# Expert tiles of 256 slots instead of 512 in a two-expert routed block on one Trainium2 core

## The chip, the cores and the metric

The kernel is one program on one core of a Trainium2 chip. The metric is the device time of one launch in microseconds (us). TensorE (PE) multiplies matrices, VectorE (DVE) does elementwise work and reductions, ScalarE (ACT) evaluates the activation functions, GpSimd (POOL) does some elementwise work and issues the gathers and scatters, and SyncE (SP) issues all other transfers. The transfers of all issuers run on the core's 16 DMA engines.

## The reference

```python
x = L0_attn_x                                    # (2, 2048, 256) float32: 4096 tokens
x = x + attention(layernorm(x))                  # 16 heads, softmax plus a local band, projection
h = layernorm(x)
rh = gelu(h @ rW1 + rb1)                         # router, 256 -> 512
probs = softmax(rh @ rW2 + rb2)                  # 4 experts
weights, indices = top_k(probs, 2)               # each token goes to 2 of 4 experts
for e in range(4):                               # We1[e]: 256 -> 1024, We2[e]: 1024 -> 256
    yo = gelu(h * token_mask[e] @ We1[e] + be1[e]) @ We2[e] + be2[e]
    out = out + yo * combine_w[e]
x = x + out
```

4096 tokens times 2 experts make 8192 pairs of a token and an expert. Only these pairs are computed.

## The kernel before

Three stages follow one another: `project` (queries, keys), `attend` (attention, to about 1455 us) and `route_and_experts`. In the third, eight blocks of 512 tokens first run through projection, layer norm and router. For each token GpSimd scatters a row of 1056 bytes (the normalised token, its four gates, its number) to two slots of a DRAM table `xs`, which has one region per expert (`scatter`). The residual stream of each block is stored to `out` (`store_residual`).

Then come the expert tiles. A tile is a run of SLOTS = 512 slots of one expert. With 8192 pairs and 4 experts at most 8192/512 + 3 = 19 tiles (MOE_TILES) are needed, and always 19 are computed. Slots past an expert's last pair hold pads, whose token number is out of bounds, so that gathers and stores skip them. `list_tiles` writes for each tile its start row and its expert to `table`: `list_early` for the first EARLY = 5 tiles, which are full after the first sequence is routed, `list_late` for the others.

For tile i SyncE's `load_tile` issues four transfers in order: `xs` (the tile's rows, into one of two buffers), the first half of the expert's weights (L996, semaphore w1_in), the second half (L1001, w2_in), and the biases (L1007). Both halves of the weights are loaded anew for every tile, as pairs of float32r pieces (high and low part), into one of two buffers `w`. From tile 2 on each issue waits until the tile before the last has left the buffer: the first half waits for all eight `hidden` of tile i-2 (h_ready), the second for all eight `output` of it (h_used), the biases for the reading of its result (y_read). Since these waits stand in one queue, each also holds back what is issued behind it.

TensorE works in steps m = 0..7, one for each 128 of the 1024 hidden features. `hidden(i, m)` (L1509) is 6 matmuls over all the tile's slots, `output(i, m)` (L1528) has 3 matmuls of 256 columns for each 128 slots, so 12 for 512 slots. A step runs `hidden(i, m+2)` and then `output(i, m)`; in steps 6 and 7 the hidden parts are those of the next tile. `tile_transposes(i+1)` (L1495) stands at m = 4. Between the two, ACT's `gelu` (L1148) and DVE's `halves` (L1319 cast, L1321 subtraction) make the high and low pieces of the hidden values. The first `gelu` of a tile waits for the tile's biases. DVE also adds the output bias, multiplies by the gate and adds the gathered rows (`add_bias` L1331, `weigh_rows` L1339, `accumulate` L1346, at m = 1, 2, 3 of the next tile), and `prepare(i+1)` (L1305 to L1312, at m = 6) reads gates and token numbers; from i+1 = 2 on it waits until tile i-1 is stored. GpSimd's order is gather tile i (`gather_rows`, L1054, one indirect DMA for each 128 slots), store tile i (`store_rows`, L1062), gather tile i+1; every gather waits until the store of the tile before has landed, since both touch `out`.

The last block's routing (logits, choice of experts, counting, slots, `list_late`) is done beside the first steps of the expert tiles: the LAST_ and LATE_ numbers say at which step.

Of the kernel before, what the change touches and what calls it, by code (L numbers as in the profile page):

```python
# [29 lines left out]
P = 128  # L30
# [5 lines left out]
BT = 4  # L36
# [28 lines left out]
SLOTS = 512  # L65
# [3 lines left out]
XS_ROWS = EXPERTS * REGION + SLOTS  # L69
# [267 lines left out]
def attend(nc, ctx, dram, keep):  # L337
# [108 lines left out]
    def _(sp):  # L446
# [379 lines left out]
def route_and_experts(nc, ctx, dram, keep, block):  # L826
# [90 lines left out]
    ends = np.cumsum([0, BT * ROW, BT * ROW, SLOTS, SLOTS, MH + DIM, MH + DIM])  # L917
# [3 lines left out]
    y = [x_sb[:, HALF * BT:HALF * BT + BT, :], attnT[:].rearrange("p k (a f) -> p (k a) f", f=DIM)]  # L921
    rows = [o_st, v_st]
# [3 lines left out]
    xT = [(xT_hi0, sb("xT_lo0", [P, KD, SLOTS], F32R)[:]), (xT_hi[:], xT_lo[:])]  # L926
    gates = [sb(f"gates{u}", [P, BT, EXPERTS]) for u in range(2)]
    gate = [sb(f"gate{u}", [P, BT]) for u in range(2)]
    token = [sb(f"token{u}", [P, BT], U32) for u in range(2)]
# [18 lines left out]
    LAST_LOGITS, LAST_GATES, LAST_SLOTS, LATE_TABLE = 0, 1, 3, 4  # L948
# [66 lines left out]
    def _(pool):  # L1015
# [57 lines left out]
        pool.wait_ge(out_stored, 16 * BT * MOE_TILES)  # L1073

    @block.scalar
    def _(act):
# [74 lines left out]
        for i in range(MOE_TILES):  # L1151
            act.wait_ge(biases_in[i % 2], 16 * (i // 2 + 1))
            for m in range(MH):
# [3 lines left out]
                if i == 0 and m == LAST_GATES:  # L1157
# [3 lines left out]
    def _(dve):  # L1161
# [140 lines left out]
        def prepare(i):  # L1302
# [3 lines left out]
                                    chosen[:, i].unsqueeze(1).broadcast_to([P, BT, EXPERTS]), ALU.mult  # L1306
                                    ).then_inc(prep_step, 1)
            if i >= 2:
                dve.wait_ge(out_stored, 16 * BT * (i - 1))
# [14 lines left out]
        def add_bias(i):  # L1324
# [4 lines left out]
            elif i >= 2:  # L1329
                dve.wait_ge(out_stored, 16 * BT * (i - 1))  # L1330
            nc.vector.tensor_tensor(y[u], ps_y[u].rearrange("p b (t f) -> p (b t) f", f=DIM),  # L1331
                                    biases[u][:, MH:].unsqueeze(1).broadcast_to([P, BT, DIM]), ALU.add
                                    ).then_inc(y_read, 1)

        def weigh_rows(i):
# [3 lines left out]
            nc.vector.tensor_tensor(y[u], y[u], gate[u][:].unsqueeze(2).broadcast_to([P, BT, DIM]), ALU.mult  # L1339
                                    ).then_inc(y_gated, 1)  # L1340

        def accumulate(i):
            u = i % 2
            dve.wait_ge(y_gated, i + 1)
            dve.wait_ge(gathered, 16 * BT * (i + 1))
# [340 lines left out]
```

## Time and profile before

| | us |
|---|---|
| median of 3 runs | 2095.99 (2094.68 to 2101.74) |
| the profiled execution's own time | 2096.47 |
| its span in the trace | 2094.7 |
| first matmul of the expert tiles | 1627.87 |
| end of the last one | about 2080.5 |
| TensorE busy over the span | 2024.2 |

The span is what the trace covers; the execution's own time is 1.8 us longer. Times in rows are counted from the span's start. The stages share the engines in different ways, so busy shares of the whole span say little about the expert tiles; the rows below are of that stage.

### The profile page before, as it was taken

How to read it: one execution, taken by the hardware profiler on the slowest of the kernel's cores; microseconds unless marked ns; L12 is line 12 of the kernel's file. 1: busy time of each engine (PE TensorE's matmuls, PEld its weight loads, DVE VectorE, ACT ScalarE, POOL GpSimd, SP SyncE). 2: the span in 40 equal slices, each digit the busy share in tenths (PEclk: the TensorE clock that was granted, in tenths of full speed). 3: DMA queues.
4: the chain of work that ended last, by engine and by line, in shares of the span. 5: the costliest groups of instructions: out<-in, count | busy, mean ns of one | idle time of the engine just before them, and what ended most of it. 6: DMA issues, size and time to landing. Idle time of an engine off the chain costs nothing. (4 is left out here: it accounts for less than half of the span.)

```text
span 2094.7 us, 48471 instructions
## 1 busy us (share of the span) xinstructions
PE 2024.2 (97%) x16588; PEld 1083.5 (52%) x16588; DVE 1647.9 (79%) x2007; ACT 1402.4 (67%) x2502; POOL 392.9 (19%) x461
## 2 busy tenths in 40 slices
PE   7899999999999999999999999998998899999997
PEld 4443333333333333333333333333886799999996
DVE  6578999999999999999999999990355555565564
ACT  3227888888888888888888888888554322222221
POOL 1243001000100100010010001000044433334333
PEclk9888999999999999999999999999999999999998
DMA  7924434533543453354335335511124666776671
GB/s 261 243 52 92 90 71 90 120 72 72 118 93 71 89 118 76 71 113 99 71 86 119 78 71 106 106 49 31 52 97 179 243 249 239 267 264 242 232 266 54
DMA packets 102092, 267.69 MB, mean 128 GB/s; under 512 B 22894, under 2 KB 45936, under 8 KB 95344
## 3 DMA queue, kind: packets, MB, share of 16 engines
q1 hardware_dynamic: 91648, 241.25, 43.4%
q0 software_dynamic: 10368, 25.45, 3.5%
q8 instruction: 45, 0.74, 0.2%
q14 instruction: 31, 0.25, 0.0%
HBM read 212.87 MB, written 74.20 MB: 137 GB/s over the span
## 5 line engine op out<-in xcount | busy, mean ns | idle before, releaser
L588 DVE TENSOR_REDUCE part_max<-psum_attend 128x1 f32<-128x1024 f32 x1024 | 1241.0, 1221 | 81.8 <-PE psum_attend L710 65.5
L643 ACT ACTIVATE probs<-psum_attend 128x512 f32<-128x512 f32 x2048 | 1110.4, 596 | 155.0 <-PE psum_attend L723 149.6
L723 PE MATMUL psum_attend<-score_q,score_k 50*128 50x512 f32 x2048 | 756.1, 452 | 1.2 <-ACT v_sb L662 0.7
L710 PE MATMUL psum_attend<-max_k,max_q 48*128 48x512 f32 x2048 | 746.4, 454 | 8.8 <-PEq L1608 6.5
L735 PE MATMUL psum_attend<-probs,v_ones 128*32 128x256 f32 x8192 | 658.1, 393 | 9.3 <-ACT heads_sb L658 8.8
L723 PEld LDWEIGHTS psum_attend<-score_q,score_k 50*128 50x128 f32 x2048 | 308.9, 186 | 409.8 <-ACT probs L643 395.9
L735 PEld LDWEIGHTS psum_attend<-probs,v_ones 128*32 128x32 f32 x8192 | 162.5, 108 | 386.0 <-issue 202.8
L710 PEld LDWEIGHTS psum_attend<-max_k,max_q 48*128 48x128 f32 x2048 | 296.9, 187 | 23.8 <-issue 13.6
L1148 ACT ACTIVATE x_sb<-psum_route,x_sb 128x512 f32<-128x512 f32 x152 | 104.5, 689 | 287.0 <-PE psum_route L1509 243.8
L1528 PE MATMUL psum_route<-w,h_hi 128*128 128x256 f32 x1216 | 218.5, 279 | 2.4 <-DVE h_lo L1321 1.3
L1528 PEld LDWEIGHTS psum_route<-w,h_hi 128*128 128x128 f32 x1216 | 195.8, 189 | 16.6 <-issue 1.7
L1319 DVE CAST h_hi<-x_sb 128x512 fp32r<-128x512 f32 x152 | 65.3, 430 | 132.8 <-ACT x_sb L1148 115.3
L1528 PE MATMUL psum_route<-w,h_lo 128*128 128x256 f32 x608 | 169.3, 278 | 0.0
L549 POOL CAST shift<-neg_max 128x16 fp32r<-128x16 f32 x31 | 6.1, 196 | 592.2 <-DVE neg_max L596 592.2
L1528 PEld LDWEIGHTS psum_route<-w,h_lo 128*128 128x128 f32 x608 | 114.7, 189 | 0.2 <-issue 0.2
L1321 DVE TENSOR_TENSOR h_lo<-x_sb,h_hi 128x512 fp32r<-128x512 f32 x152 | 105.4, 693 | 5.2
L1509 PE MATMUL psum_route<-w_end,w 128*128 128x512 f32 x320 | 102.3, 401 | 2.9 <-ACT x_sb L1148 2.9
L1509 PE MATMUL psum_route<-route_xT_hi,w 128*128 128x512 f32 x288 | 91.6, 399 | 0.0
L514 POOL COPY v_ones<-v_sb 128x256 f32<-128x256 f32 x32 | 12.7, 397 | 337.3 <-PE psum_attend L735 337.1
L1032 POOL DMA_INDIRECT xs<-xrow,slot_at x64 | 62.9, 984 | 29.9 <-issue 18.1
L559 POOL TENSOR_TENSOR o_sb<-heads_tok,inv_sum 128x256 f32<-128x256 f32 x33 | 20.4, 620 | 252.5 <-DVE inv_sum L604 221.2
L1062 POOL DMA_INDIRECT out<-x_sb,token x40 | 40.9, 1024 | 109.6 <-DVE x_sb L1346 98.4
(171 smaller groups left out, 1538.0 us busy)
## 6 DMA issues: line engine op xcount, KB each, us to landing
w<-w_split SPq DMA_DIRECT2D x38, 2048.0 KB
max_q<-qk_pieces SPq DMA_DIRECT2D x192, 128.0 KB, 7.4
score_k<-qk_pieces SPq DMA_DIRECT2D x192, 128.0 KB, 4.6
xs<-in_pads SPq DMA_DIRECT2D x33, 528.0 KB, 5.8
qk_pieces<-pieces SPq DMA_DIRECT2D x32, 512.0 KB, 4.6
w_split<-w_pair SPq DMA_DIRECT2D x32, 512.0 KB, 6.3
max_k<-qk_pieces SPq DMA_DIRECT2D x192, 64.0 KB, 7.6
score_q<-qk_pieces SPq DMA_DIRECT2D x192, 64.0 KB, 2.2
```

The costliest lines, as they stand in the source:

```text
L588: nc.vector.tensor_reduce(part_max[:, t, p:p + 1], ps_m[p].rearrange("q b f -> q (b f)"), axis=AXIS.X, op=ALU.max).then_inc(m_read, 1)
L643: nc.scalar.activation(probs[kb % 2][:, chunk * BLOCK:(chunk + 1) * BLOCK], bank_of(at), ACT.Exp, scale=float(HD) ** -0.5).then_inc(exp_do ...
L710: last = nc.tensor.matmul(ps_m[p][:, h, :], max_q[u][rows, t * P:(t + 1) * P], max_k[u][rows, p * BLOCK:(p + 1) * BLOCK], start=True, stop ...
L723: nc.tensor.matmul(bank_of(at), score_k[u][rows, kb * P:(kb + 1) * P], score_q[u][rows, part * BLOCK:(part + 1) * BLOCK], start=True, stop ...
L735: last = nc.tensor.matmul(ps_o[QUAD * j:QUAD * (j + 1), at:at + BLOCK // PARTS], v_ones[u][:, kb, :], probs[kb % 2][:, j * BLOCK + at:j * ...
L1032: nc.gpsimd.indirect_dma_start(dram["xs"], bass.IndirectOffsetOnAxis(ap=at, axis=0), xrow[i % XROWS][:, t, :], None).then_inc(scattered[i ...
L1062: nc.gpsimd.indirect_dma_start(dram["out"], bass.IndirectOffsetOnAxis(ap=token[u][:, t:t + 1], axis=0), y[u][:, t, :], None, bounds_check= ...
L1148: nc.scalar.activation(h[m % H], ps_h[m % PS_H], ACT.Gelu, bias=biases[i % 2][:, m:m + 1]).then_inc(gelu_done, 1)
L1319: nc.vector.tensor_copy(h_hi[m % HALVES], h[m % H]).then_inc(h_hi_ready, 1)
L1321: nc.vector.tensor_tensor(h_lo[m % HALVES], h[m % H], h_hi[m % HALVES].bitcast(F32), ALU.subtract).then_inc(h_lo_ready, 1)
L1509: last = nc.tensor.matmul(ps_h[m % PS_H], w[u][:, 2 * k + m // 4, c, at:at + P], xx[:, k, :], start=j == 0, stop=j == len(terms) - 1)
L1528: last = nc.tensor.matmul(ps_y[u][:, t // 2, (t % 2) * DIM:(t % 2 + 1) * DIM], hs[m % HALVES][:, toks], w[u][:, chunk, c, at:at + DIM], st ...
```

## The change

Tiles have 256 slots. There are then 8192/256 + 3 = 35 of them, and EARLY is 4096/256 - 3 = 13. Every operation over a tile's slots has half the width or half the count; weights and biases are loaded once for each tile as before. The result of a tile takes half a PSUM bank group, and `output(1, 0)` no longer shares a bank with the counting, so one wait goes. The last block's routing is spread over more steps, now counted across tiles. The filling of `xs` with pads keeps its 33 transfers of 512 rows.

```diff
-SLOTS = 512
+SLOTS = 256
+PADS = 512
...
-XS_ROWS = EXPERTS * REGION + SLOTS
+XS_ROWS = EXPERTS * REGION + PADS
...
-            sp.dma_start(dram["xs"][ds(n * SLOTS, SLOTS), :], dram["pads"]).then_inc(pads_in, 16)
+            sp.dma_start(dram["xs"][ds(n * PADS, PADS), :], dram["pads"]).then_inc(pads_in, 16)
...
-    ps_x = psum[:, 2:4, :]
-    ps_h = [psum[:, 4 + c, :] for c in range(PS_H)]
-    ps_y = [psum[:, 6:8, :], psum[:, 0:2, :]]
+    ps_x = psum[:, 2:4, 0:SLOTS]
+    ps_h = [psum[:, 4 + c, 0:SLOTS] for c in range(PS_H)]
+    ps_y = [psum[:, 6, :], psum[:, 1, :]]
...
-    LAST_LOGITS, LAST_GATES, LAST_SLOTS, LATE_TABLE = 0, 1, 3, 4
+    LAST_LOGITS, LAST_GATES, LAST_COUNT, LAST_SLOTS, LATE_TABLE = 0, 2, 3, 6, 10
...
-                pool.wait_ge(out_stored, 16 * BT * i)
+                pool.wait_ge(out_stored, 16 * ST_TILES * i)
...
-            for t in range(BT):
+            for t in range(ST_TILES):
...
-                if i == 0 and m == LAST_GATES:
+                if MH * i + m == LAST_COUNT:
                     exponentials(BLOCKS - 1)
...
-                elif m == LAST_LOGITS:
+                if MH * i + m == LAST_LOGITS:
                     read_logits(BLOCKS - 1)
-                elif m == LAST_GATES:
+                elif MH * i + m == LAST_GATES:
                     choose(BLOCKS - 1)
-                elif m == LAST_SLOTS:
+                elif MH * i + m == LAST_SLOTS:
                     weigh(BLOCKS - 1)
                     give_slots(BLOCKS - 1)
-                elif m == LATE_TABLE:
+                elif MH * i + m == LATE_TABLE:
                     list_late()
...
-                elif i == 1:
-                    pe.wait_ge(place_read, BLOCKS)
-                else:
+                elif i >= 2:
                     pe.wait_ge(y_read, i - 1)
             pe.wait_ge(h_lo_ready, s + 1)
             chunk, at = W1 + m // 2, (m % 2) * DIM
-            for t in range(BT):
+            for t in range(ST_TILES):
...
-                if i == 0 and m == LAST_GATES:
+                if MH * i + m == LAST_COUNT:
                     count_slots(BLOCKS - 1)
```

TensorE's queue around steps 0 and 1 of tile 0, before. `w_end` and `xT_lo` are the high and low pieces of the tile's transposed rows, `w` the weights, `h_hi` and `h_lo` the pieces of the hidden values.

```order
L1509 MATMUL psum_route<-w_end,w 128x512 [waits gelu_done]
L1509 MATMUL psum_route<-w_end,w 128x512
L1509 MATMUL psum_route<-xT_lo,w 128x512 x2
L1509 MATMUL psum_route<-w_end,w 128x512 x2
L1528 MATMUL psum_route<-w,h_hi 128x256 [waits h_lo_ready]
L1528 MATMUL psum_route<-w,h_hi 128x256
L1528 MATMUL psum_route<-w,h_lo 128x256
L1528 MATMUL psum_route<-w,h_hi 128x256 x2
L1528 MATMUL psum_route<-w,h_lo 128x256
L1528 MATMUL psum_route<-w,h_hi 128x256 x2
L1528 MATMUL psum_route<-w,h_lo 128x256
L1528 MATMUL psum_route<-w,h_hi 128x256 x2
```

The same place with the change (lines are numbered two higher up to `output`):

```order
L1511 MATMUL psum_route<-w_end,w 128x256 [waits gelu_done]
L1511 MATMUL psum_route<-w_end,w 128x256
L1511 MATMUL psum_route<-xT_lo,w 128x256 x2
L1511 MATMUL psum_route<-w_end,w 128x256 x2
L1528 MATMUL psum_route<-w,h_hi 128x256 [waits h_lo_ready]
L1528 MATMUL psum_route<-w,h_hi 128x256
L1528 MATMUL psum_route<-w,h_lo 128x256
L1528 MATMUL psum_route<-w,h_hi 128x256 x2
L1528 MATMUL psum_route<-w,h_lo 128x256
```

The hidden part keeps its six matmuls at half the columns; the output part keeps its 256 columns and has six matmuls for twelve.

SyncE's queue of one tile (tile 2) before, with what each transfer waits for; the names are those of `load_tile`.

```order
L992 ISA [waits prepared,x_tr]
L992 DMA x_sb<-xs 128x4x264
L996 ISA [waits h_ready]
L996 DMA w<-w_split 128x4x1024
L1001 ISA [waits h_used]
L1001 DMA w<-w_split 128x4x1024
L1007 ISA [waits y_read,gelu_done]
L1007 DMA x_sb<-in_be 128x264
```

The same with the change:

```order
L994 ISA [waits prepared,x_tr]
L994 DMA x_sb<-xs 128x2x264
L998 ISA [waits h_ready]
L998 DMA w<-w_split 128x4x1024
L1003 ISA [waits h_used]
L1003 DMA w<-w_split 128x4x1024
L1009 ISA [waits y_read,gelu_done]
L1009 DMA x_sb<-in_be 128x264
```

Order and waits are the same; only the tile's rows are halved, the two halves of the weights keep their size, and the list now stands 35 times for 19.

## Rows read from the trace of the kernel before

**Rows 1.** The page's part 1: busy us (share of the span) xinstructions of each engine.
```profile
PE 2024.2 (97%) x16588; PEld 1083.5 (52%) x16588; DVE 1647.9 (79%) x2007; ACT 1402.4 (67%) x2502; POOL 392.9 (19%) x461
```
**Rows 2.** DMA issues, 1500 us on: out<-in, queue, kind, count, KB each.
```profile
w<-w_split SPq DMA_DIRECT2D x38, 2048.0 KB
x_sb<-xs SPq DMA_DIRECT2D x19, 528.0 KB
x_sb<-in_be SPq DMA_DIRECT2D x19, 132.0 KB
```
**Rows 3.** Windows view: stretch, length, busy of PE, PEld, DVE, ACT, POOL, PEclk, DMA share, GB/s.
```profile
1800.00:1900.00 100.00, 100.00 (x660) 90.69 (x659) 58.70 (x101) 28.24 (x39) 37.99 (x36) 1.00 0.70 253
```
**Rows 4.** Timeline of SP's queue: start us, us, engine, line, operation; both weight halves.
```profile
1731.43 0.38 SPq L996 DMA_DIRECT2D w<-w_split  x1
1738.33 0.38 SPq L1001 DMA_DIRECT2D w<-w_split  x1
...
1754.42 0.38 SPq L996 DMA_DIRECT2D w<-w_split  x1
```
**Rows 5.** Windows view, shorter stretches.
```profile
1610.00:1636.00 26.00, 21.55 (x121) 15.82 (x120) 9.63 (x43) 13.37 (x17) 14.40 (x15) 0.96 1.03 405
...
1748.00:1752.00 4.00, 4.00 (x32) 3.75 (x31) 1.96 (x3) 2.08 (x3) 2.60 (x3) 1.00 0.30 109
...
1780.00:1784.00 4.00, 4.00 (x30) 3.71 (x29) 1.35 (x3) 1.38 (x2) 1.34 (x2) 1.00 1.02 411
```
**Rows 6.** Timeline of all engines inside the expert tiles.
```profile
1740.36 0.43 DVE L1319 CAST h_hi<-x_sb 128x512 fp32r<-128x512 f32 x1 [0.47 <-ACT x_sb L1148]
...
1740.75 0.63 PE L1509 MATMUL psum_route<-w_end,w 128*128 128x512 f32 x2
...
1740.82 0.69 DVE L1321 TENSOR_TENSOR h_lo<-x_sb,h_hi 128x512 fp32r<-128x512 f32 x1
...
1742.13 0.40 PE L1528 MATMUL psum_route<-w,h_hi 128*128 128x256 f32 x2
...
1742.33 0.69 ACT L1148 ACTIVATE x_sb<-psum_route,x_sb 128x512 f32<-128x512 f32 x1 [2.07 <-PE psum_route L1509]
...
1743.51 0.63 PE L1509 MATMUL psum_route<-w_end,w 128*128 128x512 f32 x2
...
1749.03 1.03 PE L1495 MATMUL psum_route<-ident_sb,x_sb 128*128 128x128 f32 x8
...
1749.82 0.71 PE L1509 MATMUL psum_route<-w_end,w 128*128 128x512 f32 x2
```
**Rows 7.** Timelines of PE and SP at the start of the expert tiles.
```profile
1607.83 10.11 SPq L996 DMA_DIRECT2D w<-w_split  x1
...
1637.01 1.22 PE L1509 MATMUL psum_route<-w_end,w 128*128 128x512 f32 x2 [2.87 <-ACT x_sb L1148]
...
1660.55 0.38 SPq L996 DMA_DIRECT2D w<-w_split  x1
```
**Rows 8.** PE's timeline and a half-microsecond window in the routing stage.
```profile
1481.91 1.93 PE L1436 MATMUL psum_route<-ident_sb,xrow 128*128 128x128 f32 x8 [1.68 <-DVE xrow L1293]
...
1482.50:1483.00 0.50, 0.50 (x5) 0.50 (x4) 0.00 (x0) 0.00 (x0) 0.00 (x0) 0.50 0.01 4
```
**Rows 9.** Timeline of the end: result of the last tile on DVE, its stores on POOL.
```profile
2080.63 1.22 DVE L1331 TENSOR_TENSOR x_sb<-psum_route,x_sb 128x1024 f32<-128x1024 f32 x1 [2.15 <-PE psum_route L1528]
...
2083.15 1.22 DVE L1346 TENSOR_TENSOR x_sb<-x_sb,o_st 128x1024 f32<-128x1024 f32 x1
2085.22 1.03 POOL L1062 DMA_INDIRECT out<-x_sb,token  x1 [3.86 <-DVE x_sb L1346]
...
2089.15 0.99 POOL L1062 DMA_INDIRECT out<-x_sb,token  x1 [0.30 <-issue]
```
**Rows 10.** Timeline of POOL: last store of a tile, first gather of the next.
```profile
1750.23 0.99 POOL L1062 DMA_INDIRECT out<-attnT,token  x1 [0.30 <-issue]
...
1753.54 1.05 POOL L1054 DMA_INDIRECT o_st<-out,token  x1 [2.33 <-DMA out<-attnT,token]
```

More of the change, by code:

```diff
@@ L916, in route_and_experts @@
     x_at = x_sb[:].rearrange("p t f -> p (t f)")
-    ends = np.cumsum([0, BT * ROW, BT * ROW, SLOTS, SLOTS, MH + DIM, MH + DIM])
+    ends = np.cumsum([0, ST_TILES * ROW, ST_TILES * ROW, SLOTS, SLOTS, MH + DIM, MH + DIM])
     xs0, xs1, h0, h1, biases0, biases1 = (x_at[:, int(a):int(b)] for a, b in zip(ends, ends[1:]))
@@ L920, in route_and_experts @@
     h, biases = [h0, h1], [biases0, biases1]
-    y = [x_sb[:, HALF * BT:HALF * BT + BT, :], attnT[:].rearrange("p k (a f) -> p (k a) f", f=DIM)]
-    rows = [o_st, v_st]
+    y = [x_sb[:, HALF * BT:HALF * BT + ST_TILES, :],
+         attnT[:].rearrange("p k (a f) -> p (k a) f", f=DIM)[:, 0:ST_TILES, :]]
+    rows = [o_st[:, 0:ST_TILES, :], v_st[:, 0:ST_TILES, :]]
     h_hi = [sb(f"h_hi{c}", [P, SLOTS], F32R)[:] for c in range(HALVES)]
@@ L925, in route_and_experts @@
     xT_hi0 = keep["w_end"][:, 0:KD * SLOTS].rearrange("p (k n) -> p k n", k=KD)
[L926 to L929, printed above, removed]
+    xT = [(xT_hi0, sb("xT_lo0", [P, KD, SLOTS], F32R)[:]), (xT_hi[:, :, 0:SLOTS], xT_lo[:, :, 0:SLOTS])]
+    gates = [sb(f"gates{u}", [P, ST_TILES, EXPERTS]) for u in range(2)]
+    gate = [sb(f"gate{u}", [P, ST_TILES]) for u in range(2)]
+    token = [sb(f"token{u}", [P, ST_TILES], U32) for u in range(2)]
     full = sb("full", [P, EXPERTS])
@@ L1072, in _ @@
             store_rows(i)
-        pool.wait_ge(out_stored, 16 * BT * MOE_TILES)
+        pool.wait_ge(out_stored, 16 * ST_TILES * MOE_TILES)
     @block.scalar
@@ L1305, in prepare @@
             nc.vector.tensor_tensor(gates[u][:], xs[u][:, :, GATE_AT:GATE_AT + EXPERTS],
[L1306 removed]
+                                    chosen[:, i].unsqueeze(1).broadcast_to([P, ST_TILES, EXPERTS]), ALU.mult
                                     ).then_inc(prep_step, 1)
             if i >= 2:
[L1309 removed]
+                dve.wait_ge(out_stored, 16 * ST_TILES * (i - 1))
             dve.wait_ge(prep_step, 2 * i + 1)
@@ L1329, in add_bias @@
             elif i >= 2:
-                dve.wait_ge(out_stored, 16 * BT * (i - 1))
-            nc.vector.tensor_tensor(y[u], ps_y[u].rearrange("p b (t f) -> p (b t) f", f=DIM),
-                                    biases[u][:, MH:].unsqueeze(1).broadcast_to([P, BT, DIM]), ALU.add
+                dve.wait_ge(out_stored, 16 * ST_TILES * (i - 1))
+            nc.vector.tensor_tensor(y[u], ps_y[u].rearrange("p (t f) -> p t f", f=DIM),
+                                    biases[u][:, MH:].unsqueeze(1).broadcast_to([P, ST_TILES, DIM]), ALU.add
                                     ).then_inc(y_read, 1)
@@ L1493, in tile_transposes @@
             for k in range(KD):
-                for t in range(BT):
+                for t in range(ST_TILES):
                     last = nc.tensor.transpose(ps_x[:, k, t * P:(t + 1) * P], xs[u][:, t, k * P:(k + 1) * P], ident[:])
@@ L1524, in output @@
             chunk, at = W1 + m // 2, (m % 2) * DIM
-            for t in range(BT):
+            for t in range(ST_TILES):
                 toks = slice(t * P, (t + 1) * P)
                 for j, (hs, c) in enumerate(((h_hi, 0), (h_hi, 1), (h_lo, 0))):
-                    last = nc.tensor.matmul(ps_y[u][:, t // 2, (t % 2) * DIM:(t % 2 + 1) * DIM],
+                    last = nc.tensor.matmul(ps_y[u][:, t * DIM:(t + 1) * DIM],
                                             hs[m % HALVES][:, toks], w[u][:, chunk, c, at:at + DIM],
-                                            start=m == 0 and j == 0 and t % 2 == 0,
-                                            stop=m == MH - 1 and j == 2 and t % 2 == 1)
+                                            start=m == 0 and j == 0 and t == 0,
+                                            stop=m == MH - 1 and j == 2 and t == ST_TILES - 1)
             last.then_inc(h_used, 1)
@@ L1648 @@
     j, e = np.arange(EXPERTS)[None, :], np.arange(EXPERTS)[:, None]
-    pads = np.zeros((SLOTS, ROW), np.float32)
+    pads = np.zeros((PADS, ROW), np.float32)
     pads[:, ID_AT] = TOKENS
```

4 lines of the change are left out of this document (2 added, 2 removed).

## The prediction

> **What bounds the kernel now.** I read the page first: TensorE is busy for 2024.2 of 2094.7 us [rows 1], but that mixes three stages, and the change touches only the last 450 us. So I went to the windows view of that stage, then to SP's queue and to the timeline of one tile. In the middle of the expert tiles TensorE is busy for 100 of 100 us at full clock, VectorE for 59, ScalarE for 28, and the 16 DMA engines for a share of 0.70, moving 253 GB/s [rows 3]. The stage is bound by TensorE, and the reader should see the second number too: the transfers have only 30% in hand. The first weight halves of two successive tiles are issued at 1731.43 and 1754.42 [rows 4]: a tile of 512 slots takes 23.0 us.
>
> Inside a tile the hidden part of a step takes 1.38 us (1740.75 to 1742.13) and the output part 1.38 us (to 1743.51) [rows 6]. That is 0.230 us for a matmul of 512 columns and 0.115 us for one of 256: time goes with the columns, and a matmul of 256 columns pays nothing for its own weight load. The eight transposes take 0.79 us (1749.03 to 1749.82) [rows 6]. So 8 x 2.76 + 0.8 = 22.9 us.
>
> **The change, part by part.** *TensorE's work.* A step of 256 slots is 6 + 6 matmuls of 256 columns, 12 x 0.115 = 1.38 us; a tile is 8 x 1.38 + 0.4 = 11.45 us. There are 35 for 19: 35 x 11.45 = 401 us against 19 x 23.0 = 437 us. The 36 us are the pads that are no longer computed (9728 slots become 8960). If nothing else were there, this would be the gain.
>
> *The transfers.* What a tile loads for its slots is halved, what it loads for its expert is not: 2 x 2048 KB of weights and 132 KB of biases [rows 2], for 11.45 us of TensorE work instead of 23. A full tile of 256 slots moves 4.19 MB of weights, 0.135 MB of biases, 0.27 MB of rows (half of 528 KB [rows 2]), and gathers and stores 256 rows of 1 KB each, 0.52 MB: 5.12 MB. In 11.45 us that is 447 GB/s. Before it was 253 [rows 3]. What can the DMA engines do? In the one long stretch in which they are never without work, 26 us at the start, they move 405 GB/s with scatters of 1 KB rows in the mix; in weights alone 411; in gathers alone 109 GB/s at a share of 0.30, so 360 for a full share [rows 5]. None reaches 447. The bound therefore passes from TensorE to the transfers. For the mix of 82% weights and 18% small rows I take 395 GB/s, between 0.82 at 405 with 0.18 at 350 (about 394) and the 405 of the long stretch: 13.0 us for a full tile, where TensorE needs 11.45.
>
> The Trainium skill, page "DMA: Bandwidth & Descriptors", section Specifications, puts HBM's limit for one core at about 358 GB/s. The trace disagrees: 405 GB/s over 26 us [rows 5]. By the page's figure the stream below would take 470 us instead of 426, and the span would be 2144 us.
>
> *Is the stream fed?* The change alters no wait, but every wait now comes twice as often. Call b the moment at which the biases of tile i are there; they are queued behind its second weight half, and the first gelu needs them. Then gelu 0 and the two operations of `halves` follow, at 256 columns between half and all of 0.69, 0.43 and 0.69 us [rows 6]; I take 0.5, 0.27 and 0.43, with 0.2 for the handovers: `output(i,0)` starts at b + 1.4. From there to `output(i,7)` TensorE has 15 parts of 0.69 and the transposes, 10.8 us: b + 12.2. The next b' is at b + 13.0. TensorE waits for about 1 us a tile. `hidden(i,7)` is done at b + 8.7, which releases the first half for tile i+2; at that time the second half of tile i+1 is still under way, to b + 12.5. The second half for tile i+2 is released at b + 12.2, with the first still before it. So something is always queued, with about 4 us in hand, and a late TensorE catches up before the queue runs dry. SP's issue can block while the queue is full (10.11 us [rows 7]); that costs nothing here, since it happens only while the engines have work.
>
> *ScalarE and VectorE.* Gelu to `halves` must fit in the four parts between `hidden(i,m)` and `output(i,m)`, 2.76 us; the chain is about 1.2 us plus 0.6 for handovers, and an extra operation of VectorE adds 0.69. It fits, with less than 1 us in hand. `prepare(i+1)` at m = 6 waits for the stores that follow `accumulate` at m = 3: 0.85 us from VectorE to GpSimd (2084.37 to 2085.22 [rows 9]), two issues 2.3, landing 2.3 (1751.22 to 1753.54 [rows 10]), together 5.5 us after `accumulate`, where three steps and the split are about 4.5. VectorE stalls there for about 1 us, up to 3 if stores land late beside weights. TensorE's 1 us of waiting hides the first; the rest would come on top only if it passed the 4 us above in every tile. I cost it at nothing and keep 13.6 us a tile as the upper end (rival 3).
>
> *The clock.* After a wait of TensorE of 1.68 us the granted clock was 0.50, its level of 1.2 GHz [rows 8]. With a wait in every tile this can happen. A slow stretch makes TensorE late, the wait vanishes, and so does the cause; as long as the transfers bound the tile it costs nothing.
>
> *The start.* Before, `hidden(0,2)` starts at 1637.01 and the first weight half of tile 2 is issued at 1660.55 [rows 7]: 23.5 us, of which six steps are 16.6 and about 7 are the last block's routing, the slow clock there and stalls. With the change six steps are 8.3 us and I keep the 7: with the start 0.5 us earlier, 1652. If the spreading hides all the 7 it is 1645, if it costs 12 it is 1657. The late table and the waits of tile 1 fall in the time in which tile 2 is loaded; I add 1 us for a gap in the stream, and 1 us until the first bytes flow.
>
> *The sum.* From there the tiles 2 to 34 are one stream: 33 x (4.194 + 0.135 + 0.270) = 151.8 MB, and 16.3 MB of the 16.8 MB that 8192 pairs gather and store: 168.1 MB at 395 GB/s are 425.6 us. The stream ends at 1652 + 2 + 425.6 = 2079.6, b is 0.5 later. Then 1.4 us to the first output part, 13 parts of 0.69 = 9.0, three VectorE operations of 0.69 with 0.2 between them, 0.85 to GpSimd, 2.3 for two stores, and 4.6 from there to the end as before (2090.14 to 2094.7 [rows 9]): 20.4 us. The span is 2100.5, against 2094.7; with the 1.8 us around it the time is 2102. The profiled execution took 2096.47, the median is 2095.99, so nothing is to be corrected. The gain of TensorE, 36 us, is thus all given back and 6 us more.
>
> **The rivals.**
> 1. *The stream is faster, and the kernel too.* This decides from 408 GB/s on. For it: 411 in weights alone and 405 in the long mix [rows 5]. Against it: stretches with gathers beside weights are below that. At 409 GB/s the stream is 411 us, and with a start at 1650 the span is 2084, the time 2086.
> 2. *The stream is slower.* In steady state 253 GB/s at a share of 0.70 are 361 GB/s for a full share [rows 3], because a transfer holds its engines while it starts and ends. If back-to-back transfers keep that loss, 168.1 MB take 466 us, and the time is 2142. Against it: the long stretch has the same starts and ends and reaches 405. At 380, half way, the time is 2119.
> 3. *The step chain or the stores bound the tile.* VectorE's wait for `out_stored`, with late landings and a slow clock, makes a tile 13.6 us and leaves gaps in the stream: 33 x 13.6 = 449, the time 2125. For it: the chain has less than 1 us in hand, the clock fell after 1.68 us [rows 8]. Against it: the 4 us that are queued ahead.
> 4. *The change does only what it says:* TensorE stays the bound with 11.45 us a tile, the time is 2062. It needs 447 GB/s, more than any row shows.
>
> **How the numbers follow.** Forecast (the transfers bound at about 395 GB/s, 2093 to 2111): 0.45. Rival 1: 0.18. Rival 2: 0.17. Rival 3: 0.15. Rival 4: 0.02. Left over 0.03. A measurement of this kernel can tell 0.3%, 6.3 us: same is 2089.7 to 2102.3. The forecast lies at its upper edge, so of its 0.45 I give 0.20 to same and 0.25 to slower; of rival 1 0.15 to faster and 0.03 to same; rivals 2 and 3 are slower but for 0.01 each. Slower 0.56, same 0.25, faster 0.19. The range leaves out rival 4 and the far end of rival 2: 2083 to 2130; the forecast's own is 2093 to 2111.
>
> **What would show it.** Right: in the middle of the expert tiles the DMA share is near 1 and 385 to 405 GB/s, the first weight halves are issued 12.6 to 13.4 us apart, TensorE is busy for 85 to 92 of 100 us and waits once a tile, at the biases or w2_in. The first half for tile 2 is issued between 1645 and 1657, and from the last second half to the end there are about 21 us. Wrong: TensorE busy for 100 of 100 (rival 4, or the chain), a DMA share of 0.9 or less with longer tiles (rival 3), a share of 1 at 360 GB/s (rival 2).

## The result, and the profile after

The changed kernel takes 2238.65 us (median of 4 runs, 2224.51 to 2249.21), the one before beside it 2095.34 (2086.1 to 2101.74): a ratio of 1.067, with an interval of 1.063 to 1.072. I had forecast 2102, with a range to 2130. The sign was right; of 143 us lost I had foreseen 6.

The page of the changed kernel first: part 1, one issue line, part 4 (the chain that ended last) and the group of part 5 that stands for `prepare`.

```profile
PE 2055.6 (92%) x17200; PEld 1147.1 (51%) x17200; DVE 1682.4 (75%) x2375; ACT 1432.8 (64%) x2646; POOL 388.3 (17%) x449
...
DMA 10%; issue 3%; POOL 2%; DVE 1%; PE 0%; POOLq 0%; ACT 0%; DVEq 0%
...
L1313 DVE TENSOR_REDUCE gate<-gates 128x2 f32<-128x8 f32 x35 | 5.6, 161 | 140.5 <-DMA out<-x_sb,token 72.3
...
w<-w_split SPq DMA_DIRECT2D x70, 2048.0 KB
```

TensorE's share has gone from 97% [rows 1] to 92%, there are 70 weight halves for 38 [rows 2], and TensorE has 0% of the chain that ended last. VectorE stands idle for 140.5 us before 35 tiny reductions that cost 5.6: they are the ones behind `prepare`'s wait, the wait that I had costed at nothing. It is about the size of the loss.

SP's queue at the start and the end of the stream:

```profile
1653.68 0.38 SPq L998 DMA_DIRECT2D w<-w_split  x1
...
2194.18 0.38 SPq L998 DMA_DIRECT2D w<-w_split  x1
```

The stream starts where it was expected (1653.68, forecast 1652). From there to the first half of tile 34 are 540.5 us for 32 tiles: 16.9 us a tile, not 13.0. The windows view in between (columns as in [rows 3]):

```profile
1700.00:2200.00 500.00, 399.61 (x2951) 391.36 (x2952) 250.23 (x684) 129.70 (x266) 128.69 (x120) 0.89 0.83 300
```

This is the picture that I had named for rival 3: a DMA share under 0.9 with longer tiles. Nothing is full. TensorE works 80% of the time, the transfers 83%, at 300 GB/s. When no engine is the bound, the next thing to look for is a loop of waits. The timelines of POOL and DVE for one turn of it, with the idle time and its releaser in brackets:

```profile
1778.51 1.17 POOL L1056 DMA_INDIRECT v_st<-out,token  x1 [5.48 <-DVE token L1314]
1779.97 1.13 POOL L1056 DMA_INDIRECT v_st<-out,token  x1 [0.30 <-issue]
1788.19 1.03 POOL L1064 DMA_INDIRECT out<-attnT,token  x1 [7.09 <-DVE attnT L1348]
1789.53 1.00 POOL L1064 DMA_INDIRECT out<-attnT,token  x1 [0.31 <-issue]
```

```profile
1777.65 0.16 DVE L1313 TENSOR_REDUCE gate<-gates 128x2 f32<-128x8 f32 x1 [5.10 <-DMA out<-x_sb,token]
...
1786.67 0.69 DVE L1348 TENSOR_TENSOR attnT<-attnT,v_st 128x512 f32<-128x512 f32 x1 [2.15 <-DMA v_st<-out,token]
...
1795.28 0.16 DVE L1313 TENSOR_REDUCE gate<-gates 128x2 f32<-128x8 f32 x1 [5.22 <-DMA out<-attnT,token]
```

From one `gate` to the next are 17.6 us: 0.86 to the first gather, 2.59 for two issues, **5.57 until the gathered rows have landed**, 0.69 for `accumulate`, 0.83 to GpSimd, 2.34 for two stores, **4.75 until they have landed**. Tile i+1 cannot be gathered before tile i is stored, and tile i cannot be stored before it was gathered, so the loop turns once a tile whatever TensorE does. The profile names VectorE's `token` as what releases the gather, because it comes last; by the code the gather and `gate` wait for the same landing, and the 0.86 us are GpSimd's own start. Before, the loop also turned once a tile, but a tile lasted 23 us, and the gather came 2.33 us after the last store [rows 10], where here it comes 5.60 us after (1790.53 to 1796.13).

That this loop closes can be read from `accumulate`: it waits for its gathered rows in nearly every tile. Waits view, 1650 to 2238 (engine, tile and line, releaser: us in total, times, longest):

```profile
DVE x_sb L1348 <- DMA o_st<-out,token: 36.9, 17, 3.6
...
DVE attnT L1348 <- DMA v_st<-out,token: 33.1, 15, 3.9
```

What it does to TensorE: VectorE, held at `gate`, has the next pieces of the hidden values behind it. The same view:

```profile
PE psum_route L1528 <- DVE h_lo L1323: 107.3, 41, 6.3
...
DVE gate L1313 <- DMA out<-x_sb,token: 72.3, 16, 7.9
DVE gate L1313 <- DMA out<-attnT,token: 68.0, 16, 6.5
```

PE's timeline at the turn shown above, and windows of one microsecond before and after:

```profile
1796.22 0.80 PE L1528 MATMUL psum_route<-w,h_hi 128*128 128x256 f32 x2 [3.62 <-DVE h_lo L1323]
```

```profile
1794.00:1795.00 1.00, 0.00 (x0) 0.00 (x0) 0.00 (x0) 0.00 (x0) 0.00 (x0) 1.00 1.03 418
1797.00:1798.00 1.00, 1.00 (x7) 1.00 (x6) 0.89 (x3) 0.00 (x0) 0.69 (x2) 0.50 0.53 205
```

At 1794 TensorE, VectorE, ScalarE and GpSimd all stand still until one store has landed, while the weights of a later tile run at 418 GB/s. After 3.62 us of idle time the granted clock is 0.50, TensorE's level of 1.2 GHz, as after the 1.68 us of [rows 8]. The mean over 500 us is 0.89.

### The profile page after: what moved, and what is told of

Same layout as the page of the kernel before. It is cut to its first block and busy times, and to the rows that moved or that the text cites. A ratio compares the mean times of both kernels' runs of the same rounds, so it can differ in the third digit from the quotient of the medians.

```text
span 2238.0 us, 50903 instructions
## 1 busy us (share of the span) xinstructions
PE 2055.6 (92%) x17200; PEld 1147.1 (51%) x17200; DVE 1682.4 (75%) x2375; ACT 1432.8 (64%) x2646; POOL 388.3 (17%) x449
## 5 line engine op out<-in xcount | busy, mean ns | idle before, releaser
L1150 ACT ACTIVATE x_sb<-psum_route,x_sb 128x256 f32<-128x256 f32 x280 | 132.9, 475 | 406.7 <-PE psum_route L1511 240.1
L1528 PE MATMUL psum_route<-w,h_hi 128*128 128x256 f32 x1120 | 238.5, 307 | 111.7 <-DVE h_lo L1323 107.3
L1321 DVE CAST h_hi<-x_sb 128x256 fp32r<-128x256 f32 x280 | 88.6, 316 | 60.5 <-ACT x_sb L1150 53.6
L1511 PE MATMUL psum_route<-w_end,w 128*128 128x256 f32 x576 | 126.5, 304 | 2.7 <-ACT x_sb L1150 2.7
L1323 DVE TENSOR_TENSOR h_lo<-x_sb,h_hi 128x256 fp32r<-128x256 f32 x280 | 120.1, 429 | 9.7
L1511 PE MATMUL psum_route<-route_xT_hi,w 128*128 128x256 f32 x544 | 118.4, 301 | 1.3 <-ACT x_sb L1150 1.3
L1313 DVE TENSOR_REDUCE gate<-gates 128x2 f32<-128x8 f32 x35 | 5.6, 161 | 140.5 <-DMA out<-x_sb,token 72.3
L1511 PEld LDWEIGHTS psum_route<-w_end,w 128*128 128x128 f32 x576 | 98.2, 209 | 3.9 <-ACT x_sb L1150 2.9
L1511 PEld LDWEIGHTS psum_route<-route_xT_hi,w 128*128 128x128 f32 x544 | 92.0, 208 | 1.5 <-ACT x_sb L1150 1.5
L515 POOL COPY v_ones<-v_sb 128x256 f32<-128x256 f32 x32 | 12.7, 397 | 336.8 <-PE psum_attend L736 336.7
```

The costliest lines, as they stand in the source:

```text
L1150: nc.scalar.activation(h[m % H], ps_h[m % PS_H], ACT.Gelu, bias=biases[i % 2][:, m:m + 1]).then_inc(gelu_done, 1)
L1321: nc.vector.tensor_copy(h_hi[m % HALVES], h[m % H]).then_inc(h_hi_ready, 1)
L1323: nc.vector.tensor_tensor(h_lo[m % HALVES], h[m % H], h_hi[m % HALVES].bitcast(F32), ALU.subtract).then_inc(h_lo_ready, 1)
L1511: last = nc.tensor.matmul(ps_h[m % PS_H], w[u][:, 2 * k + m // 4, c, at:at + P], xx[:, k, :], start=j == 0, stop=j == len(terms) - 1)
L1528: last = nc.tensor.matmul(ps_y[u][:, t * DIM:(t + 1) * DIM], hs[m % HALVES][:, toks], w[u][:, chunk, c, at:at + DIM], start=m == 0 and j = ...
```

## The experiments

**Without the round trip.** Stores go to a table of their own, gathers don't wait for them, and four buffers of token numbers take `prepare`'s wait away. The store itself now waits for the store before it.

```diff
-    token = [sb(f"token{u}", [P, ST_TILES], U32) for u in range(2)]
+    token = [sb(f"token{u}", [P, ST_TILES], U32) for u in range(4)]
...
-                pool.wait_ge(out_stored, 16 * ST_TILES * i)
...
+            if i > 0:
+                pool.wait_ge(out_stored, 16 * ST_TILES * i)
...
-                nc.gpsimd.indirect_dma_start(dram["out"],
+                nc.gpsimd.indirect_dma_start(dram["acc"],
...
-            if i >= 2:
-                dve.wait_ge(out_stored, 16 * ST_TILES * (i - 1))
+            if i >= 4:
+                dve.wait_ge(out_stored, 16 * ST_TILES * (i - 3))
```

> From the changed kernel: the tiles' results are stored to a tensor of their own, while the gathers read `out`, which after the routing nobody writes any more; so a gather no longer waits for the store before it (the store itself waits, before it is issued, until the one before has landed), and four buffers of gates and token numbers take away VectorE's wait in `prepare`. It leaves out that the two experts' results of a token are added up. Same transfers, same bytes, same engine work. Theory A (the tile is bound by the ring gather, landing, accumulate, store, landing, prepare, gather, 17.1 us): with the ring cut the transfers bound the tile at 13.0 us, time 2095 to 2115 us, DMA share near 1 at 390 to 405 GB/s. Theory B (the DMA engines give only about 360 GB/s in this mix): 14.2 us a tile, about 2142 us, share near 1 at 360 GB/s. Theory C (TensorE's step chain and its clock bound the tile): no change, about 2239 us.

Measured: 2120.15 us, ratio to before 1.009 (1.005 to 1.012). Its windows view:

```profile
1700.00:2080.00 380.00, 357.43 (x2905) 350.19 (x2904) 245.24 (x668) 124.69 (x261) 122.44 (x117) 0.99 1.00 390
```

Here is the kernel that I had predicted: 13.07 us a tile in the median (forecast 13.0), a DMA share of 1.00, 390 GB/s (forecast 395), TensorE at 94%. The round trip therefore costs about 2239 - 2120 = 119 us of the 143, and the stream most of the rest.

**Each wait alone.** First the kernel in full with four token buffers: `prepare` no longer waits, the gather still does.

```diff
-    token = [sb(f"token{u}", [P, ST_TILES], U32) for u in range(2)]
+    token = [sb(f"token{u}", [P, ST_TILES], U32) for u in range(4)]
```

> From the changed kernel: four buffers of gates and token numbers in place of two, so that `prepare` waits for the store of tile i-4 and not of tile i-2; nothing else. Theory A: the ring stays closed by the gather's own wait for the store before it, only VectorE's step in it goes (about 1 us): 16 to 16.8 us a tile, time 2205 to 2230 us. Rival theory D (the stall of VectorE in `prepare` is the cause, since it holds back the hidden values and with them TensorE and the loads): without it 13.0 to 13.5 us a tile, time 2100 to 2120 us.

Then the reverse: stores go to the other table, so the gather doesn't wait, but `prepare` still does, with two buffers.

```diff
-                pool.wait_ge(out_stored, 16 * ST_TILES * i)
...
+            if i > 0:
+                pool.wait_ge(out_stored, 16 * ST_TILES * i)
...
-                nc.gpsimd.indirect_dma_start(dram["out"],
+                nc.gpsimd.indirect_dma_start(dram["acc"],
```

> As the kernel without the round trip (results stored to a tensor of their own, gathers wait for no store; it too leaves out the adding up of the two experts), but with two buffers of gates and token numbers, so that VectorE's `prepare` waits for the store again. Theory A1 (only the ring through the gather's wait binds the tile): 13.0 us a tile, time about 2120 us. Theory A2 (there is a second ring, through VectorE's order: accumulate 0.7, to GpSimd 0.8, two issues 2.3, landing 4.8, prepare, then five steps of 1.38 us to the next accumulate): about 16 us a tile, time 2200 to 2225 us; then each of the two rings alone keeps most of the loss, and only taking both away gives it back.

Measured: 2206.88 us, ratio 1.050 (1.046 to 1.054), in theory A's range, and 2154.83 us, ratio 1.027 (1.021 to 1.032), between the two theories and fitting neither: with the gather free, `prepare`'s wait alone still costs something, but far less than a second loop of 16 us. With the other two kernels this is a square:

| ratio to before | gather doesn't wait | gather waits |
|---|---|---|
| `prepare` doesn't wait | 1.009 | 1.050 |
| `prepare` waits | 1.027 | 1.067 |

The windows view of the kernel in which only `prepare` waits:

```profile
1700.00:2080.00 380.00, 338.23 (x2684) 333.03 (x2684) 226.81 (x618) 117.19 (x241) 112.07 (x107) 0.96 0.98 359
```

Its DMA share is 0.98 at 359 GB/s, where the kernel without both waits has 1.00 at 390: a share near 1 does not mean that the transfers are at their best. In the changed kernel the window 1791 to 1792, just after a weight half was issued, has a share of 0.96 and moves 70 GB/s. The gather's wait costs about 4 per cent with or without the other, `prepare`'s about 1.8. The larger one, which the prediction never priced, is not in the long idle time of `gate` by itself: with `prepare` free, the idle time moves to the gathers. Waits view of the kernel with four token buffers, 1700 to 2080:

```profile
DVE x_sb L1348 <- DMA o_st<-out,token: 82.3, 13, 8.6
POOL o_st L1056 <- DMA out<-attnT,token: 67.0, 12, 6.6
```

**A quarter of the weights, with the round trip and without.** From tile 2 on each weight half loads 512 KB in place of 2048.

```diff
-            sp.dma_start(w[u][:, 0:W1].bitcast(F32),
+            part = W1 if i < 2 else 1
+            sp.dma_start(w[u][:, 0:part].bitcast(F32),
```

> From the changed kernel: from tile 2 on each half of the weights is loaded to a quarter only (0.5 MB for 2.1 MB); the rest of the buffer keeps the weights of tiles 0 and 1, so these tiles compute with wrong weights. All waits and all gathers and stores stay. Theory A: the gathers and stores land in 2.3 us again instead of 5 to 6, the ring is 0.9 + 2.6 + 2.3 + 0.7 + 0.8 + 2.3 + 2.3 = 12 us, TensorE's 11.5 to 12.2 us bound the tile, time 2055 to 2080 us. Theory B gives the same here. Theory C: the tile stays at 17 us, time above 2200 us.

> Leaves out that a gather sees the stores before it (they go to a table of their own) and loads a quarter of the weights from tile 2 on, so neither the ring nor the stream can bound. Theory A (TensorE would hold 11.45 us a tile without these two): 33 tiles take 378 us, the gain of 36 us on TensorE appears, the time is 2055-2070 and TensorE is busy for 98 of 100 us. Rival (a third limit, the chain gelu, cast, subtraction to the output part, keeps the 12.2-12.6 us a tile that the light weights alone showed): 33 x 12.4 = 409 us, the time is 2085-2100 with TensorE waiting at h_lo.

Measured with the round trip: 2106.64 us, ratio 1.002 (0.999 to 1.005), outside what I had expected. Without: 2079.03 us, ratio 0.992 (0.989 to 0.996), also 9 us above the expected range. Windows view of the latter:

```profile
1700.00:2000.00 300.00, 300.00 (x2542) 299.88 (x2541) 219.63 (x585) 109.47 (x229) 105.96 (x101) 1.00 0.52 165
```

TensorE is at last the bound. Its timeline, at the first matmuls of two successive steps:

```profile
1802.80 0.40 PE L1512 MATMUL psum_route<-route_xT_hi,w 128*128 128x256 f32 x2
...
1804.22 0.40 PE L1512 MATMUL psum_route<-route_xT_hi,w 128*128 128x256 f32 x2
```

A step takes 1.42 us for the 1.38 assumed, a tile 11.83, not 11.45. The weight loads (second number) fill the time as well, 299.88 of 300; whether they are the 3% is not shown. So the gain of 36 us on TensorE's side was worth 18 (2096.6 for the kernel before, less 2079.0) even with every other limit out of the way.

With light weights but the round trip, the median from the last store to `gate` is 1.47 us, and `accumulate` starts 3.1 us after the last gather is issued (1700 to 2060, 28 turns). In 15 of these turns it doesn't wait for the gather at all, so that is an upper bound of that landing. The loop is then at most 0.86 + 2.59 + 3.1 + 0.69 + 0.83 + 2.34 + 1.47 = 11.9 us: in quiet it just fits beside TensorE's 11.83. It has nothing in hand, though: in 8 of the 28 turns `gate` comes 2.5 to 3.7 us after the store, the mean tile is 12.7 us, and the time stays 28 us above that without the round trip. With full weights the mean tile is 16.9 us. The landings beside the weights are what grew.

**Why the landings are long.** In the changed kernel's trace I set each landing beside the last weight issue before it. Of eleven groups of stores from 1720 to 1900, six had a weight half issued 0.6 us before their last issue ended and one 0.3: they landed in 4.2 to 6.0 us. Three had no weight half ahead of them closer than 9.8 us and landed in 1.5 us, although one was issued 0.1 to 0.7 us behind. One with a half 0.2 us ahead landed in 1.5 too. All eleven gathers had one 0.6 to 1.4 us ahead and took 5.2 to 5.9. With halves of a quarter of the size in the same place, 0.5 to 0.6 us ahead, stores landed in 3.3 to 3.4 us. The turn shown above is one of the long stores: SP issued a half at 1789.95, the last store ended its issue at 1790.53. One turn later, POOL's, SP's and DVE's timelines, a short one (1807.82 to 1809.28):

```profile
1806.82 1.00 POOL L1064 DMA_INDIRECT out<-x_sb,token  x1 [0.30 <-issue]
```

```profile
1808.51 0.38 SPq L998 DMA_DIRECT2D w<-w_split  x1
```

```profile
1809.28 0.16 DVE L1313 TENSOR_REDUCE gate<-gates 128x2 f32<-128x8 f32 x1 [0.81 <-DMA out<-x_sb,token]
```

Two theories: Q, a small transfer waits for the bytes queued ahead of it; R, it takes turns with the rows of the weights, whatever is queued. Four kernels, each in full, try what shortens it.

Rows of half the size, in twice the transfers:

```diff
+            for s in range(2):
+                sp.dma_start(w[u][:, 0:W1, s, :].bitcast(F32),
```

> From the changed kernel: each weight half is loaded by two transfers, of the high and of the low pieces, so that its rows are 2 KB and not 4 KB; same bytes, same waits. In the changed kernel a store's last row lands 4.8 us after its issue and a gather's 5.6 us, where it is 2.3 us without weights beside it. Theory R (rows of the small transfers and of the weights take turns on each DMA engine, so the delay goes with the size of a weight row): landings of about 3.8 us, a tile of 14.5 to 15.5 us for 16.9, time 2155 to 2195 us. Theory Q (the delay goes with the bytes of weights that are queued): landings stay at about 5 us and the time at 2230 us or above, more if smaller rows make the weights slower.

Measured: 2221.07 us, ratio 1.059 (1.054 to 1.065), 16.0 us a tile; from store to `gate` 4.0 us, from gather to `accumulate` 5.5. That is between the two ranges. The effect is small, and its interval meets that of the changed kernel (1.063 to 1.072): the size of the weights' rows is not what decides.

The first weight half waits for the stores:

```diff
+            if i >= 3:
+                sp.wait_ge(out_stored, 16 * ST_TILES * (i - 2))
```

> From the changed kernel: SyncE issues the first weight half of tile i only once the store of tile i-3 has landed, which is one wait more. Theory A with its cause of the late landings (a store shares the engines with the 2 MB that are issued beside it): stores land in 2.3 us instead of 5, the ring is 15 us, time 2160 to 2200 us: a wait more makes the kernel faster. Rival (the landing is late whatever runs beside it, or the stream is the bound): nothing gained and the stream has one more gap a tile, 2240 to 2290 us.

Measured: 2225.29 us, ratio 1.058 (1.053 to 1.062). A wait more made the kernel 0.6% faster by the medians, far less than expected: the store then lands in 3.7 us, but both halves, issued 3.3 and 1.4 us ahead of the gather, now stand before that (5.3 us).

Pieces of 1 MB, at most two queued:

```diff
+        def load_pieces(i, u, expert, first):
+            for q in range(first, first + 2):
+                before = 4 * i + q - 2
+                if before >= 0:
+                    sp.wait_ge(piece_in[before % 4], 16 * (before // 4 + 1))
```

> The full computation, with the weights in pieces of 1 MB of which at most two are queued at once. Theory Q (a small gather or store waits for the bytes of weights queued ahead of it): with 2 MB or less queued instead of up to 4 MB both landings shorten, gather from 5.6 to about 4 us and store from 4.7 to about 3.5, the ring goes from 17.6 to 14.5-15.5 us, the time is 2160-2200. Theory R (the small rows take turns with the weights row by row, whatever is queued): landings stay at 5.6 and 4.7 us as long as any weights run, the tile stays 16.5-17 us and the time is 2230 or more; the pacing can only add gaps.

Measured: 2193.82 us, ratio 1.048 (1.041 to 1.056), as theory Q had it. The gather lands in 4.5 us, the store in 3.6 (medians, 1700 to 2060), a tile takes 15.3. The transfers are busier for it:

```profile
1700.00:2080.00 380.00, 322.97 (x2463) 317.73 (x2462) 209.75 (x568) 108.00 (x221) 106.47 (x99) 0.91 0.90 333
```

Both weight halves wait, so that only one is ever ahead of a small transfer:

```diff
+            if i >= 3:
+                sp.wait_ge(out_stored, 16 * ST_TILES * (i - 2))
...
+                sp.wait_ge(gathered, 16 * ST_TILES * (i - 1))
```

> The full computation with two waits more on SyncE's queue: the first weight half of tile i is issued only when the stores of tile i-3 have landed, and the second only when the gathers of tile i-2 have landed too, so that at most one half is queued ahead of a small transfer. Theory Q (a small transfer waits for the weights that were issued before it, about 5 us for 2 MB): the gather comes 3.3 us behind the first half and lands in 2.5-3.5 us in place of 5.2, the store meets only the rest of the second half and lands in 2-3 us, the ring is 0.9 + 2.6 + 3 + 0.7 + 0.8 + 2.3 + 2.5 = 12.8, with the waits of the weights 13.3-14.5 us a tile: 2120-2160. Rival (the landings are long whenever weights flow, whatever is ahead, and waits on the weights only take from the stream): 5 and 4 us of landing, 16 us a tile or more, 2210-2240.

Measured: 2274.67 us, ratio 1.086 (1.083 to 1.089), the slowest of all. Both theories had it faster than this. SP's timeline, and windows between the two issues:

```profile
1782.68 0.38 SPq L1000 DMA_DIRECT2D w<-w_split  x1
1791.20 0.38 SPq L1006 DMA_DIRECT2D w<-w_split  x1
```

```profile
1783.00:1784.00 1.00, 0.57 (x4) 0.57 (x5) 0.88 (x3) 0.83 (x2) 0.66 (x1) 1.00 0.41 34
1784.00:1785.00 1.00, 1.00 (x8) 1.00 (x7) 0.97 (x4) 0.00 (x0) 0.70 (x2) 0.66 0.69 127
...
1786.00:1787.00 1.00, 1.00 (x7) 1.00 (x7) 0.69 (x3) 0.18 (x1) 0.00 (x0) 0.50 0.95 369
...
1791.00:1792.00 1.00, 1.00 (x11) 1.00 (x10) 0.90 (x2) 0.42 (x1) 0.00 (x0) 1.00 0.00 0
```

A weight half that follows a gap moves little for its first 2 us, then runs at about 400 GB/s and is done after 8, not after 5 as I had reckoned. The gather, whose issue ended 3.1 us behind it, lands 5.3 us later, and each wait on the stream opens a gap of 2 us in it. The start of a transfer, which in a fed queue is hidden, is paid twice a tile. The changed kernel pays it too, while its stores are under way; the half was issued at 1789.95:

```profile
1790.00:1791.00 1.00, 1.00 (x10) 1.00 (x10) 0.06 (x1) 0.28 (x1) 0.53 (x1) 1.00 0.21 53
1791.00:1792.00 1.00, 1.00 (x11) 1.00 (x10) 0.00 (x0) 0.47 (x1) 0.00 (x0) 1.00 0.96 70
```

The run in which both halves wait does not decide between Q and R: once a half takes 8 us, a gather 3.1 us behind it that waits for all of it lands after 5, as it did. What speaks against Q in its simple form is the changed kernel, where the stores of 1790.53 land at 1795.28, before the half ahead of them is through (the DMA share is 1.05 until 1797 and 0.53 after). By what rule the two share the engines stays open.

**Two repairs together.** Paced weights and four token buffers:

> The full computation with tiles of 256, paced weights and four token buffers together. If the time goes with the ring alone, as its sum says: the paced ring of 15.3 us loses the way through VectorE's prepare (2.6 us between store landing and gather, of which about 0.3 stays), 13.1-13.9 us a tile, near the 13.07 that the stream of weights allows: 2125-2150. If the two repairs save the same thing (landings are short only because the stream has gaps, and get long again as the tiles shorten): 14.5-15.3 us a tile, 2170-2195.

Measured: 2196.44 us, ratio 1.043 (1.038 to 1.048), against 1.048 for pacing and 1.050 for the buffers alone; the three intervals overlap. The second branch held, within 2 us of its range: the repairs save mostly the same time. Its reason did not show: the trace has 15.4 us a tile and 4.6 us from gather to `accumulate`, beside 15.2 and 4.5 with pacing alone (1700 to 2060). Neither did the tiles get shorter nor the landings clearly longer. Why the buffers add nothing to pacing stays open.

**A mix of sizes.** 13 tiles of 512, as many as are always full, and 9 of 256, one between each two of the later big ones, with four token buffers. It computes 8960 slots, like the changed kernel, and loads 22 times weights for 35.

```diff
+SIZES = [SLOTS] * EARLY + [HALF_SLOTS, SLOTS] * (BIG - EARLY) + [HALF_SLOTS] * (SMALL - BIG + EARLY)
+STS = [n // P for n in SIZES]
```

> A version that should beat both: 13 tiles of 512 slots and 9 of 256 in place of 19 of 512 (8960 slots for 9728), all five early ones of 512, then one of 256 and one of 512 in turn; four buffers of gates and token numbers. It computes the whole reference. Theory A (a tile of 256 slots pays only where the weights of the next tile and the ring have the time of a large tile beside them): TensorE stays the bound with 13 x 23.0 + 9 x 11.5 = 402 us for 437, a few us of it lost to the routing of the last block and to the rings, time 2065 to 2085 us, against 2096 to 2103 for the kernel before. If the rings of a small tile (17 us) and of a large one (20 to 23 us) add up, the pair takes 37 to 40 us for 34.5 and the time is 2085 to 2110 us.

Measured: 2094.13 us, ratio 1.000 (0.998 to 1.002). No change, as the second branch had it: from the gather of one big tile to that of the next are 38.1 us (mean of seven, 36.7 to 40.0; the 37.2 that I put into the next expectation is a typical pair, not the mean) where TensorE has 34.5. The loop adds over the pair; POOL's timeline has a big tile's last store and the gather behind it, 7.9 us later:

```profile
1885.07 0.98 POOL L1072 DMA_INDIRECT out<-x_sb,token  x1 [0.30 <-issue]
1893.96 1.04 POOL L1064 DMA_INDIRECT v_st<-out,token  x1 [7.91 <-DMA out<-x_sb,token]
```

So I put the paced weights into it:

> The full computation: 13 tiles of 512 and 9 of 256 as in the mixed kernel, with the weights in pieces of 1 MB of which at most two are queued. In the mixed kernel a pair 512 + 256 took 37.2 us (and up to 39.4) where TensorE needs 34.5, its ring being two landings of gathers (5.7 and 5.6) and two of stores (2.3 and 7.9 us). Theory Q (the small transfers wait for the weights queued ahead, as the paced kernel of 256 slots showed: 5.6 to 4.5 and 4.7 to 3.3 us): the ring of a pair loses 3 to 5 us, TensorE bounds most pairs, nine of them give back 15-25 us: 2070-2085. Rival: the pair is bound by something that pacing does not touch, or the pacing makes weights late in the small tiles: 2090-2100, no change.

Measured: 2090.36 us, beside 2102.24 for the kernel before: ratio 0.994 (0.991 to 0.997), the only full kernel here that comes out ahead of the one before, by 0.6%. That is a small gain at most: the median of the kernel before, measured anew beside each group of runs, itself lay between 2090.87 and 2103.56. The trace doesn't show it either: a pair takes 37.9 us, in an execution of 2102.47 us, the second longest of eleven. The expected 2070 to 2085 were missed, since the long landings stay; two of the gathers behind a big tile's stores:

```profile
1869.68 1.05 POOL L1069 DMA_INDIRECT v_st<-out,token  x1 [7.64 <-DMA out<-x_sb,token]
...
1941.65 1.04 POOL L1069 DMA_INDIRECT v_st<-out,token  x1 [6.40 <-DMA out<-x_sb,token]
```

## Why the prediction was wrong

*TensorE's work, the start, the stream: right, with small errors.* A tile of TensorE's work is 11.83 us for 11.45, the stream starts at 1653.7 for 1652, and where nothing else holds it back it runs at 390 GB/s for 395 and gives 13.07 us a tile for 13.0. The Trainium skill's limit of 358 GB/s ("DMA: Bandwidth & Descriptors", Specifications), which I had set aside, doesn't bind here either, with one core running: 390 over 380 us. With the round trip gone, 2120 was measured for 2102; of that residue 3 us are the start (1655.30 there) and 11 the stream, whose 32 tiles took 13.35 us on average with the slower first ones. It is within the range. Two terms were added up slightly wrong, without effect: the mix gives 395 and not 394 GB/s, and the parts of the end add up to 20.6 and not 20.4 us.

*"ScalarE and VectorE": the step that failed.* I wrote "landing 2.3", and costed `prepare`'s wait at nothing. Three things were wrong with it:
- The 2.3 us [rows 10] were read in a quiet moment, and they count to the next gather, GpSimd's start of 0.86 us with them. The window of 1748 to 1752, which I quoted for gathers and which in truth holds the stores, shows a DMA share of 0.30 [rows 5]; over the landing itself it is 0.16 (1751.20 to 1753.50). My own forecast said that the share would be 1 from now on; the duration had to be read where that is so. From last store to gather it became 5.60, of which 4.75 are the landing; a gather's landing became 5.57.
- I followed the stores as far as VectorE's stall and stopped there. The gather behind them, and its landing, were in no sum, though the gather's wait alone is worth 4%. The loop gather, accumulate, store, gather has to be closed and compared with the tile: even with 2.3 for the gather's landing it is 2.59 + 2.3 + 0.69 + 0.83 + 2.34 + 2.33 = 11.1 us. That fits into the 13.0 forecast with only 1.9 us in hand for two landings, and these took 6.5 more.
- "The rest would come on top only if it passed the 4 us": VectorE's stall is 140.3 us over 32 waits, 4.4 us a tile, not 1, and above the 3 that I had allowed for late stores. A margin of queued work covers a delay once. It does not cover one that returns in each turn.

The kernel before had a warning in it. Once in its expert tiles a store landed late, with a weight half issued 1.2 us behind it (at 2008.43): the gather came 4.37 us after the store, and `gate` waited for 3.2 us. POOL's timeline, the waits view from 1700 to 2080, and the windows view of the quiet landing and of this one:

```profile
2011.60 1.37 POOL L1054 DMA_INDIRECT v_st<-out,token  x1 [4.37 <-DVE token L1312]
```

```profile
DVE gate L1311 <- DMA out<-x_sb,token: 3.2, 1, 3.2
```

```profile
1751.20:1753.50 2.30, 2.30 (x18) 2.13 (x17) 2.27 (x4) 0.69 (x1) 0.01 (x1) 1.00 0.16 57
...
2007.00:2012.00 5.00, 5.00 (x35) 4.50 (x33) 1.74 (x7) 1.38 (x2) 0.63 (x2) 1.00 0.57 170
```

One case doesn't show a cause, but it was a late landing in the kernel before, and that at a share of only 0.57.

*"Is the stream fed?" and "The clock": failed with it.* With 16.9 us a tile the queue runs dry (share 0.83), and TensorE's granted clock falls to a mean of 0.89 over 500 us, in slow stretches that I had taken to be harmless under a bound of transfers. Whether they lengthen the tile is not shown: `accumulate`, which TensorE's work must also reach in time, waited for the gather in 32 tiles. How much of the 119 us is the clock I did not separate.

*Rival 3* had the mechanism, including late landings and the falling clock, at 0.15 and with 13.6 us a tile. Its price was a stall of 3 us at one wait; the measured tile is 3.3 us longer than that. The chance was too small and the price had no bound from the rows, because none of them showed a small transfer beside a full stream; the upper end of an unseen landing should have been the time of a weight half itself, some 5 us, which the sum 0.86 + 2.6 + 5 + 0.7 + 0.8 + 2.3 + 5 = 17.3 would have turned into 2102 + 33 x 4.3 = 2244.

*Rivals 1 and 4* fell: a stream that nothing held back ran at 390 GB/s, not 408, and TensorE was not the bound. *Rival 2's* 361 GB/s at a full share turned up (359 at 0.98), but as the sign of a wait, not as the transfers' limit.

## What to carry to other kernels

When tiles shrink, list every loop of waits that turns once a tile (here gather, add, store, gather), sum it with its landings, and compare it with the new tile; the busy shares don't show it until it binds. Take each landing from a stretch as busy as the one that you forecast, and if there is none, bound it by the time of the large transfer that will stand before it. Waits on a bulk stream that are to protect small transfers can cost more than they save, since each gap in the stream pays a transfer's start anew.

## What the runs showed of the hardware

- A store of 256 rows of 1 KB lands in about 1.5 us when no load of 2 MB was issued in the 9 us before it, and in 4.2 to 6.0 when one was issued 0.3 to 0.6 us ahead; one with a load 0.2 us ahead landed in 1.5 too. Gathers with such a load 0.6 to 1.4 us ahead took 5.2 to 5.9 (eleven of each, changed kernel). In the kernel in which both weight halves wait, with the load 3.1 to 3.7 us ahead, they took 4.8 to 6.2. With loads of 512 KB in place of 2 MB the median was at most 3.1; with nothing beside it no run shows a gather.
- The same stream of weights and rows runs at 390 GB/s for 380 us with a DMA share of 1.00. A weight half after a gap moves 34 and 127 GB/s in the first two windows, 53 and 70 in the changed kernel.
- With 256 columns everywhere, weight loads busy for 299.88 of 300 us and a step 3% longer than in the kernel before, where such matmuls alternate with others of 512 columns.
